# A graph layer on one Trainium2 core: a 16-bit table of places read in halves, and the residual input transferred behind the last super

## The chip, the cores and the metric

The kernel runs on one NeuronCore of a Trainium2 chip. The metric is device time in microseconds (us) of one execution; three executions of the kernel before gave 801.4, 800.42 and 801.16 us, median 801.16.

## The reference

There are 6250 nodes of 256 features (`x`) and 100,000 edges of 64 features. For every node the edges whose `src` it is are averaged; a two-layer MLP takes the node, this mean and a global vector; the result is added to `x` (the residual) and normalised.

```
sums   = segment_sum(edge_attr, src, 6250);  counts = segment_sum(1, src, 6250)
agg    = sums / max(counts, 1)
h      = relu(concat([x, agg, u[0]]) @ W1 + b1)          # hidden 512
out    = layernorm(x + h @ W2 + b2)                      # rows of 256
```

`dst` plays no part in the result.

## The kernel before, in words

All five engines have a program of their own, written out by hand, and meet at semaphores. The work has three stages.

**Sorting (to about 450 us).** Edges are taken in 44 chunks of 18 tiles of 128. TensorE sorts them with one-hot matmuls (L858) into groups of 4 edges of the same bucket (25 buckets of 250 nodes), ScalarE evacuates them, and GpSimd writes them with indirect DMAs (L600) to `sorted_rows` in HBM. Beside it TensorE makes the first layer's product of `x` (L785). VectorE works out a table `where` with two values per super (L1197 to L1220): its first half holds for each super the column in PSUM to which its sums go (the place, used by TensorE), its second half the row of `sorted_rows` at which each pair of supers begins (used by SyncE). SyncE writes it to HBM (L483) and reads it back as one row of one partition, `where_row` (L493), here with 32-bit elements.

**Supers (about 452 to 671 us).** A super is 128 rows of `sorted_rows`; there are 258, in 129 pairs. For each pair SyncE transfers 396 KB into one of 8 buffers `sup` (L511), as soon as TensorE is done with the pair that lay there (`s_added`, L510). VectorE compares node numbers for three or four of its four slots (L1236), ScalarE does the fourth slot of every second super (L713, L716): that gives `onehot`, of which there are 4 buffers. TensorE adds up each super with 24 matmuls of 64 or 65 columns, each with a weight load of its own (L936), into PSUM at a column that only the table knows. TensorE's program is a loop of 16 turns of 16 supers (`super_turn`, L926, called in the loop at L942 and once more at L944 for the last 2 supers). A turn starts with one `pe.load` of the 16 places into 16 registers (L927). In each super `pe.snap` makes an address of a register (L929), the sequencer waits for `s_hot_d` (L930) and in every second super for `s_hot_a` (L932), and the matmuls follow.

SyncE's program goes in turns of 8 pairs: `find_rows` loads 8 registers with the pairs' rows (L503), and 8 transfers follow. Turns 0 to 2 are written out, turns 3 to 14 are a loop (L524), turns 15 and 16 are written out again (turn 16 has one pair). The residual input `x` goes into `xs` in 12 pieces of 4 columns (two DMAs each, L527, behind the supers of turns 3 to 14) and a last one of 2 columns (L531, behind turn 15). `XPART` splits each piece into partitions 0 to 111 and 112 to 124.

**Output (about 671 us to the end).** 25 steps of two node columns: transposes of the means, the edges' part of layer one (L972, L974), relu on ScalarE, the second layer (L990), `y + xs` on VectorE (L1296), the moments, the normalisation on ScalarE (L748), and the store by SyncE (L538). Before `xs` is used, GpSimd adds `b2` to it (`add_b2`, L619); it does so for 3 steps ahead before the steps begin, and then for step g + 3 in step g. It waits once for all of `xs` (L614).

Of the kernel before, what the change touches and what calls it, by code (L numbers as in the profile page):

```python
# [9 lines left out]
I32 = mybir.dt.int32  # L10
U32 = mybir.dt.uint32
U16 = mybir.dt.uint16
# [5 lines left out]
P = 128  # L18
NODES, DIM = 6250, 256
# [5 lines left out]
NP = 125  # L25
COLS = NODES // NP
BUCKETS = COLS // 2
ROW = FEAT + 1
XPART = 112
# [35 lines left out]
SUPER_PAIRS = -(-SUPERS // 2)  # L65
ZERO_SUPER = 2 * SUPER_PAIRS
# [7 lines left out]
SUPER_COLS = -(-SUPERS // P)  # L74
# [19 lines left out]
PAIR_BUFS = 8  # L94
HOT_BUFS = 4
BODY = 2 * PAIR_BUFS
SUP_TURNS = SUPER_PAIRS // PAIR_BUFS
ACT_SLOT = SLOTS - 1
TURN = 3
TURNS = CHUNKS // TURN  # L100
# [5 lines left out]
LOOKS = -(-(BATCHES - SOON) // LOOK)  # L106
assert LOOKS + 3 <= CHUNKS

X_TURN = 3
X_COLS = 4  # L110
X_PIECES = COLS // X_COLS
X_PIECE = X_COLS * DIM
B2_AHEAD = 3
Z_BUFS = 3
assert X_TURN + X_PIECES + 1 == SUP_TURNS

STEPS = COLS // 2
PAIR = 10
# [4 lines left out]
def build(nc, x, src, attr, u, w1, b1, w2, b2, out):  # L123
# [1 line left out]
    first_d = nc.dram_tensor("first_d", [BATCHES, E1], U8, kind="Internal").ap()  # L125
    jump_d = nc.dram_tensor("jump_d", [BATCHES, E1], U16, kind="Internal").ap()
    clear_d = nc.dram_tensor("clear_d", [CLEARS * P], U32, kind="Internal").ap()
    where_d = nc.dram_tensor("where_d", [2, SUPER_COLS * P], I32, kind="Internal").ap()
    src_main = src[0:FULL * P].rearrange("(p t) -> p t", p=P)
    attr_main = attr[0:FULL * P, :].rearrange("(p t) f -> p (t f)", p=P)  # L130
    x_v = x.rearrange("(p c) d -> p (c d)", p=NP)
# [4 lines left out]
    with ctx:  # L136
        def sb(name, shape, dt=F32):
            return ctx.enter_context(nc.sbuf_tensor(name, shape, dt))

        def edge_sb(name, shape, dt=F32):  # L140
            return edge_ctx.enter_context(nc.sbuf_tensor(name, shape, dt))
# [4 lines left out]
        def sem(name):  # L146
            return ctx.enter_context(nc.semaphore(name))

        ident = sb("ident", [P, P])
        b2_all = sb("b2_all", [P, DIM])  # L150
        eps_col = sb("eps_col", [P, 1])
        where_row = sb("where_row", [1, 2 * SUPER_COLS * P], I32)
        node_of = sb("node_of", [P, 2 * P], I16)
        pre = sb("pre", [P, COLS * HID // P * NP])
        stats = sb("stats", [P, 2, 2, 6])
# [56 lines left out]
        bank_at = edge_sb("bank_at", [P, SUPER_COLS])  # L212
        column = edge_sb("column", [P, SUPER_COLS])
        beyond = edge_sb("beyond", [P, SUPER_COLS])
        where = edge_sb("where", [P, 2, SUPER_COLS], I32)
        chosen = edge_sb("chosen", [P, SOON * E1])
        edge_ctx.close()

# [56 lines left out]
        xs = sb("xs", [P, COLS * DIM])  # L275
# [88 lines left out]
        s_apart = sem("s_apart")  # L364
        s_added = sem("s_added")
        s_table = sem("s_table")
        s_xs = sem("s_xs")
        s_xb = sem("s_xb")
        s_own_act = sem("s_own_act")
        s_own_dve = sem("s_own_dve")  # L370
# [33 lines left out]
        def _(sp):  # L404
# [97 lines left out]
            def find_rows(m, count=PAIR_BUFS):  # L502
                sp.load(row_regs[0:count], where_row[0:1, bass.ds(m * PAIR_BUFS + SUPER_COLS * P, count)])  # L503

            def super_turn(m, count=PAIR_BUFS, found=False):
                if not found:
                    find_rows(m, count)
                for k in range(count):
                    at = sp.snap(row_regs[k], min_val=0, max_val=ZERO_SUPER * P)
                    sp.wait_ge(s_added, m * BODY + (2 * k + 2))  # L510
                    sp.dma_start(sup_pair[k][:, :, :, :].rearrange("p s r w -> p s (r w)"),  # L511
                                 sorted_rows[bass.ds(at, 2 * P), :].rearrange("(s p) w -> p s w", p=P)
                                 ).then_inc(s_sup[k], 16)
# [4 lines left out]
                sp.wait_ge(s_sent[s], 16 * CHUNKS)  # L518

            super_turn(0, found=True)  # L520
            for m in range(1, X_TURN):
                super_turn(m)
            sp.wait_ge(s_pre, COLS + 1)
            with sp.Fori(X_TURN, X_TURN + X_PIECES) as m:  # L524
                super_turn(m)
                for lo, hi in ((0, XPART), (XPART, NP)):
                    sp.dma_start(xs[lo:hi, bass.ds(m * X_PIECE - X_TURN * X_PIECE, X_PIECE)],  # L527
                                 x_v[lo:hi, bass.ds(m * X_PIECE - X_TURN * X_PIECE, X_PIECE)]).then_inc(s_xs, 16)
            super_turn(X_TURN + X_PIECES)
            for lo, hi in ((0, XPART), (XPART, NP)):  # L530
                sp.dma_start(xs[lo:hi, X_PIECES * X_PIECE:COLS * DIM], x_v[lo:hi, X_PIECES * X_PIECE:COLS * DIM]  # L531
                             ).then_inc(s_xs, 16)
            super_turn(SUP_TURNS, SUPER_PAIRS - SUP_TURNS * PAIR_BUFS)

            def store_step(g, b):
                sp.wait_ge(s_out, g * 2 + 2)
# [10 lines left out]
        def _(pool):  # L547
# [63 lines left out]
                pool.wait_ge(s_w_hi, 3)  # L611
                nc.gpsimd.tensor_tensor(low, whole, high.bitcast(F32), ALU.subtract).then_inc(s_w_lo, 1)
            pool.wait_ge(s_b2, 16)
            pool.wait_ge(s_xs, 2 * 16 * (X_PIECES + 1))  # L614

            def add_b2(g):
                for c in range(2 * g, 2 * g + 2):
                    column_x = xs[0:NP, c * DIM:(c + 1) * DIM]
                    nc.gpsimd.tensor_tensor(column_x, column_x, b2_all[0:NP, :], ALU.add).then_inc(s_xb, 1)  # L619

            for g in range(B2_AHEAD):
                add_b2(g)
# [9 lines left out]
            for g in range(STEPS):  # L632
                low_hidden(g, g % 2)
                if g + B2_AHEAD < STEPS:
                    add_b2(g + B2_AHEAD)

        @block.scalar
        def _(act):
# [70 lines left out]
            def super_turn(m, count=BODY):  # L709
                for k in range(0, count, 2):  # L710
                    act.wait_ge(s_sup[k // 2], m * 16 + 16)
                    act.wait_ge(s_added, m * BODY + (k + 1 + SUP_FREE - HOT_BUFS))
                    nc.scalar.activation(apart[k // 2 % 2][:, :], node_of[:, :], ACT.Abs, scale=-1.0,  # L713
                                         bias=place_in[k][:, ACT_SLOT, :]).then_inc(s_apart, 1)
                    act.wait_ge(s_apart, m * PAIR_BUFS + (k // 2 + 1))
                    nc.scalar.activation(onehot[k % HOT_BUFS][:, ACT_SLOT, :], apart[k // 2 % 2][:, :], ACT.Relu, scale=-1.0,  # L716
                                         bias=1.0).then_inc(s_hot_a, 1)

            with act.Fori(0, SUP_TURNS) as m:
                super_turn(m)  # L720
            super_turn(SUP_TURNS, 2 * SUPER_PAIRS - SUP_TURNS * BODY)

# [46 lines left out]
        def _(pe):  # L769
# [153 lines left out]

            table_regs = [pe.alloc_register(f"table_reg{k}") for k in range(BODY)]

            def super_turn(m, count=BODY):  # L926
                pe.load(table_regs[0:count], where_row[0:1, bass.ds(m * BODY, count)])  # L927
                for k in range(count):
                    at = pe.snap(table_regs[k], min_val=0, max_val=(PAIR_BANKS - 1) * 1024 + (BANK_COLS - 1) * ROW)  # L929
                    pe.wait_ge(s_hot_d, m * BODY + (k + 1))  # L930
                    if k % 2 == 0:
                        pe.wait_ge(s_hot_a, m * PAIR_BUFS + (k // 2 + 1))  # L932
                    for r in range(SLOTS):
                        for h in range(2):
                            for part, width in ((0, FEAT), (1, FEAT), (2, ROW)):
                                last = nc.tensor.matmul(ps[:, bass.ds(at + h * 512, width)],  # L936
                                                        onehot[k % HOT_BUFS][:, r, h * P:(h + 1) * P],
                                                        sup[k][:, r, part * PLANE:part * PLANE + width],
                                                        start=False, stop=False)
                    last.then_inc(s_added, 1)  # L940

            with pe.Fori(0, SUP_TURNS) as m:  # L942
                super_turn(m)
            super_turn(SUP_TURNS, 2 * SUPER_PAIRS - SUP_TURNS * BODY)  # L944
            for k in range(BANKS):
                last = nc.tensor.matmul(table_p[k], zeros[:, :], zeros[:, 0:1].to_broadcast([P, table_p[k].shape[1]]),
# [408 lines left out]
```

## Time and profile before

| | |
|---|---|
| runs | 801.4, 800.42, 801.16 us, median 801.16 |
| profiled execution's span, first to last instruction | 799.5 us |
| TensorE matmuls busy | 745.1 us, 93% of the span |
| VectorE busy | 716.8 us, 90% |
| ScalarE, GpSimd busy | 501.7 us, 63%; 417.1 us, 52% |
| HBM traffic | 195 GB/s over the span |
| stage of the supers | about 452 to 671 us |

The page does not say which of the three times belongs to the profiled execution; what lies around the span is 0.9 to 1.9 us. Busy shares are means over the three stages, and a matmul counts as busy from its start to its modelled end, so matmuls that are started 31 ns apart and are 193 ns long give a busy TensorE throughout. Times of single instructions on a sequencer (loads of registers, branches, waits) are not in the busy times; they have rows of their own, marked with a q (PEldq is TensorE's sequencer, SPq is SyncE's).

### The profile page before, as it was taken

What the parts mean: (1) busy time and instruction counts of PE and PEld (TensorE: products, weight loads), DVE (VectorE), ACT (ScalarE), POOL (GpSimd) and SP (SyncE); (2) the same over time, 40 slices, a digit from 0 to 9 for tenths busy, and PEclk for the clock granted to TensorE, in tenths of its full rate; (3) what the DMA queues carried; (4) which work ended last, traced back from release to release, by engine and by line L of the source; (5) the groups of instructions that cost most, each with busy time, mean ns of one, the idle gap of its engine ahead of it and who ended that gap; (6) DMA issues with size and microseconds to landing.
All of it is one profiled execution on the core that took longest, in us unless ns stands there. A gap on an engine that the chain in (4) does not pass through costs nothing.

```text
span 799.5 us, 31269 instructions
## 1 busy us (share of the span) xinstructions
PE 745.1 (93%) x11398; PEld 711.5 (89%) x11399; DVE 716.8 (90%) x2382; ACT 501.7 (63%) x998; POOL 417.1 (52%) x410
## 2 busy tenths in 40 slices
PE   8889999999999999999999888989898986899995
PEld 4689999999999999999999888989898986899995
DVE  8999999999999999999896388989898988799995
ACT  1366676666667767667667545555555552688886
POOL 3087777777677787877776400000000002788983
PEclk9999999999999999999999999999999999999999
DMA  6366556666665666656674678999999990012122
GB/s 215 131 210 204 201 202 211 213 215 219 202 219 195 212 220 211 225 205 214 203 210 167 239 227 260 281 282 282 285 283 285 281 277 10 27 52 64 53 66 64
DMA packets 75268, 156.38 MB, mean 196 GB/s; under 512 B 11084, under 2 KB 51277, under 8 KB 75097
## 3 DMA queue, kind: packets, MB, share of 16 engines
q1 hardware_dynamic: 58328, 102.33, 42.5%
q0 software_dynamic: 16896, 53.54, 17.9%
q8 instruction: 18, 0.29, 0.2%
q14 instruction: 26, 0.20, 0.1%
HBM read 95.47 MB, written 60.37 MB: 195 GB/s over the span
## 4 chain that ended last, share of the span: by engine, by line
PE 60%; DVE 30%; issue 5%; ACT 2%; POOL 1%; DMA 1%; DVEq 0%; ACTq 0%; SPq 0%; POOLq 0%
PE ps L858 33%; DVE onehot L1236 18%; PE ps L785 11%; PE ps L936 5%; PE ps L990 3%; DVE pre L1275 2%; DVE perm L1146 2%; DVE stats L1301 1%; DVE weights_z L1296 1%; PE ps L776 1%; PE ps L792 1%; POOL h_low L628 1%; PE ps L811 1%; PE ps L843 1%; PE ps L841 1%
## 5 line engine op out<-in xcount | busy, mean ns | idle before, releaser
L600 POOL DMA_INDIRECT sorted_rows<-payload,idx x264 | 304.8, 1155 | 131.8 <-issue 51.9
L858 PE MATMUL ps<-attr_buf,perm 128*128 128x198 bf16 x3168 | 302.6, 252 | 1.1 <-ACT attr_buf L642 0.8
L858 PEld LDWEIGHTS ps<-attr_buf,perm 128*128 128x128 bf16 x3168 | 288.6, 96 | 6.1 <-ACT attr_buf L642 1.2
L649 ACT CAST payload<-ps 128x792 bf16<-128x792 f32 x264 | 217.9, 825 | 76.7 <-PE ps L858 62.2
L1146 DVE TENSOR_SCALAR perm<-place_of,pos 128x512 bf16<-128x512 int16 x792 | 241.1, 362 | 3.4 <-PE ps L858 2.7
L1236 DVE TENSOR_SCALAR onehot<-node_of,sup 128x256 bf16<-128x256 int16 x903 | 192.4, 284 | 41.9 <-PE ps L936 22.3
L936 PE MATMUL ps<-sup,onehot 128*128 128x64 bf16 (+1 forms) x6192 | 196.1, 193 | 24.7 <-DVE onehot L1236 21.0
L936 PEld LDWEIGHTS ps<-sup,onehot 128*128 128x128 bf16 x6192 | 193.5, 98 | 27.3 <-issue 27.3
L619 POOL TENSOR_TENSOR xs<-xs,b_all 125x256 f32<-125x256 f32 x50 | 37.6, 775 | 209.4 <-DMA xs<-in_x 209.4
L713 ACT ACTIVATE apart<-node_of,sup 128x256 bf16<-128x256 int16 x129 | 65.6, 508 | 94.3 <-PE ps L936 90.2
L785 PE MATMUL ps<-xt,w1x 128*128 128x125 f32 x800 | 99.9, 278 | 5.9 <-DVE pos L1067 3.3
L785 PEld LDWEIGHTS ps<-xt,w1x 128*128 128x128 f32 x800 | 93.2, 192 | 10.8 <-issue 4.6
L660 ACT ACTIVATE pre<-ps,hid_bias 128x125 f32 (+1 forms) x200 | 56.7, 368 | 61.7 <-PE ps L785 61.7
L628 POOL TENSOR_TENSOR h_low<-pre,h_high 128x500 fp32r<-128x500 f32 x50 | 62.8, 1278 | 32.7 <-ACT pre L737 32.7
L1056 DVE TENSOR_TENSOR attr_buf<-attr_buf 128x576 f32<-128x576 f32 x88 | 65.8, 749 | 7.8 <-DMA attr_buf<-in_edge_attr 7.8
L1062 DVE TENSOR_TENSOR attr_buf<-attr_buf 128x576 f32<-128x576 f32 x88 | 65.4, 744 | 0.0
L716 ACT ACTIVATE onehot<-apart 128x256 bf16<-128x256 bf16 x129 | 53.8, 417 | 4.1
L990 PE MATMUL ps<-w_high,h_high 128*125 128x256 f32 x200 | 49.8, 282 | 1.0 <-issue 0.5
L990 PE MATMUL ps<-w_low,h_high 128*125 128x256 f32 x200 | 49.5, 280 | 0.0
L990 PE MATMUL ps<-w_high,h_low 128*125 128x256 f32 x200 | 34.1, 292 | 7.6 <-POOL h_low L628 7.6
L990 PEld LDWEIGHTS ps<-w_high,h_high 128*125 128x125 f32 x200 | 37.1, 185 | 1.3 <-issue 0.7
L990 PEld LDWEIGHTS ps<-w_low,h_high 128*125 128x125 f32 x200 | 37.2, 186 | 0.0
(150 smaller groups left out, 603.7 us busy)
## 6 DMA issues: line engine op xcount, KB each, us to landing
sup<-sorted_rows SPq DMA_DIRECT2D x129, 396.0 KB, 4.0
attr_buf<-in_edge_attr SPq DMA_DIRECT2D x43, 576.0 KB
out<-weights_z SPq DMA_DIRECT2D x25, 224.0 KB
xs<-in_x SPq DMA_DIRECT2D x12, 448.0 KB
x_stage<-in_x SPq DMA_DIRECT2D x47, 112.0 KB
sorted_rows<-payload,idx POOLq DMA_INDIRECT x264
pre<-jump_d SPq DMA_DIRECT2D x1, 1560.0 KB, 10.4
pre<-first_d SPq DMA_DIRECT2D x1, 780.0 KB, 7.2
```

The lines of the kernel that those rows point to most:

```text
L600: pool.indirect_dma_start(out=sorted_rows, out_offset=bass.IndirectOffsetOnAxis(ap=idx[:, n:n + 1], axis=0), in_=payload[s][:, :], in_offs ...
L628: nc.gpsimd.tensor_tensor(h_r[b][1][:, at:end], pre[:, g * KH * NW + at:g * KH * NW + end], h_r[b][0][:, at:end].bitcast(F32), ALU.subtrac ...
L649: nc.scalar.copy(payload[s][:, :].rearrange("p (r w) -> p r w", w=PART), slots_p[s % PSUM_BUFS]).then_inc(s_pay, 1)
L713: nc.scalar.activation(apart[k // 2 % 2][:, :], node_of[:, :], ACT.Abs, scale=-1.0, bias=place_in[k][:, ACT_SLOT, :]).then_inc(s_apart, 1)
L785: last = nc.tensor.matmul(pre_p[b][:, k * NP:(k + 1) * NP], w1x[:, c, k * P:(k + 1) * P], xt[b][:, c, :], start=(c == 0), stop=(c == KX - 1))
L858: last = nc.tensor.matmul(slot_p[s % PSUM_BUFS][r].rearrange("p (h f) -> p h f", f=PLANE), places, parts(a, t * CB + s), start=(t == 0 and ...
L936: last = nc.tensor.matmul(ps[:, bass.ds(at + h * 512, width)], onehot[k % HOT_BUFS][:, r, h * P:(h + 1) * P], sup[k][:, r, part * PLANE:pa ...
L990: last = nc.tensor.matmul(y_p[b][0:NP, c * DIM:(c + 1) * DIM], h_r[b][part][:, at:at + NP], w2r[w_part][:, k * DIM:(k + 1) * DIM], start=( ...
L1056: nc.vector.tensor_tensor(left, whole, high, ALU.subtract).then_inc(s_rest, 1)
L1062: nc.vector.tensor_tensor(low, left, middle, ALU.subtract).then_inc(s_low, 1)
L1146: last = nc.vector.tensor_scalar(perm[s][:, t, :], place_of[:, :], pos[:, bass.ds(c * CT + (t * CB + s), 1)], None, ALU.is_equal)
L1236: last = nc.vector.tensor_scalar(onehot[k % HOT_BUFS][:, r, :], node_of[:, :], place_in[k][:, r, :], None, ALU.is_equal)
```

## The change

The table `where`, its copy in HBM and `where_row` become 16-bit, and `where_row` is allocated first in SBUF. TensorE loads its places in halves of 8: the first half before the loop, then within each turn, ahead of super 4, the places of supers 8 to 15 of this turn, and ahead of super 12 the places of supers 0 to 7 of the next. A turn begins without a load, and the last 2 supers have none either. SyncE still loads 8 rows at the start of each turn, from the 16-bit table; its turns 1 to 15 are one loop, without DMAs of `xs` in it. Behind the last super SyncE issues `xs` in 5 pieces of 10 columns, two DMAs each, with a semaphore for each piece, and GpSimd waits for a piece when it comes to its first column.

```diff
+AHEAD = PAIR_BUFS // 2
...
-X_TURN = 3
-X_COLS = 4
+X_COLS = 10
...
-    where_d = nc.dram_tensor("where_d", [2, SUPER_COLS * P], I32, kind="Internal").ap()
+    where_d = nc.dram_tensor("where_d", [2, SUPER_COLS * P], U16, kind="Internal").ap()
...
+        where_row = sb("where_row", [1, 2 * SUPER_COLS * P], U16)
         ident = sb("ident", [P, P])
         b2_all = sb("b2_all", [P, DIM])
         eps_col = sb("eps_col", [P, 1])
-        where_row = sb("where_row", [1, 2 * SUPER_COLS * P], I32)
...
-        where = edge_sb("where", [P, 2, SUPER_COLS], I32)
+        where = edge_sb("where", [P, 2, SUPER_COLS], U16)
...
-        s_xs = sem("s_xs")
+        s_xs = [sem(f"s_xs{k}") for k in range(X_PIECES)]
...
             super_turn(0, found=True)
-            for m in range(1, X_TURN):
+            with sp.Fori(1, SUP_TURNS) as m:
                 super_turn(m)
+            super_turn(SUP_TURNS, SUPER_PAIRS - SUP_TURNS * PAIR_BUFS)
+
             sp.wait_ge(s_pre, COLS + 1)
-            with sp.Fori(X_TURN, X_TURN + X_PIECES) as m:
-                super_turn(m)
+            for k in range(X_PIECES):
                 for lo, hi in ((0, XPART), (XPART, NP)):
-                    sp.dma_start(xs[lo:hi, bass.ds(m * X_PIECE - X_TURN * X_PIECE, X_PIECE)],
-                                 x_v[lo:hi, bass.ds(m * X_PIECE - X_TURN * X_PIECE, X_PIECE)]).then_inc(s_xs, 16)
-            super_turn(X_TURN + X_PIECES)
-            for lo, hi in ((0, XPART), (XPART, NP)):
-                sp.dma_start(xs[lo:hi, X_PIECES * X_PIECE:COLS * DIM], x_v[lo:hi, X_PIECES * X_PIECE:COLS * DIM]
-                             ).then_inc(s_xs, 16)
-            super_turn(SUP_TURNS, SUPER_PAIRS - SUP_TURNS * PAIR_BUFS)
+                    sp.dma_start(xs[lo:hi, k * X_PIECE:(k + 1) * X_PIECE], x_v[lo:hi, k * X_PIECE:(k + 1) * X_PIECE]
+                                 ).then_inc(s_xs[k], 16)
...
-            pool.wait_ge(s_xs, 2 * 16 * (X_PIECES + 1))
...
             def add_b2(g):
+                if g % (X_COLS // 2) == 0:
+                    pool.wait_ge(s_xs[g // (X_COLS // 2)], 2 * 16)
                 for c in range(2 * g, 2 * g + 2):
...
+            def find_tables(half, at):
+                pe.load(table_regs[half * PAIR_BUFS:(half + 1) * PAIR_BUFS], where_row[0:1, bass.ds(at, PAIR_BUFS)])
+
             def super_turn(m, count=BODY):
-                pe.load(table_regs[0:count], where_row[0:1, bass.ds(m * BODY, count)])
                 for k in range(count):
+                    if k == PAIR_BUFS - AHEAD:
+                        find_tables(1, m * BODY + PAIR_BUFS)
+                    if k == BODY - AHEAD:
+                        find_tables(0, m * BODY + BODY)
                     at = pe.snap(table_regs[k], min_val=0, max_val=(PAIR_BANKS - 1) * 1024 + (BANK_COLS - 1) * ROW)
...
+            find_tables(0, 0)
             with pe.Fori(0, SUP_TURNS) as m:
                 super_turn(m)
```

## Rows read from the trace of the kernel before

**Rows 1.** The page: its first line and its busy times.
```profile
span 799.5 us, 31269 instructions
PE 745.1 (93%) x11398; PEld 711.5 (89%) x11399; DVE 716.8 (90%) x2382; ACT 501.7 (63%) x998; POOL 417.1 (52%) x410
```

**Rows 2.** Stretches without and with `xs`: engines' busy us, clock, DMA share, GB/s.
```profile
470.00:495.00 25.00, 23.73 (x767) 23.54 (x765) 22.59 (x108) 14.47 (x32) 0.00 (x0) 1.00 0.79 237
500.00:650.00 150.00, 136.01 (x4364) 134.70 (x4361) 133.69 (x637) 84.13 (x182) 0.00 (x0) 1.00 0.93 284
```

**Rows 3.** Timeline, TensorE's matmuls in the supers: start, us, idle before.
```profile
469.79 11.99 PE L936 MATMUL ps<-sup,onehot 128*128 128x64 bf16 x384 [1.29 <-DVE onehot L1236]
483.05 12.03 PE L936 MATMUL ps<-sup,onehot 128*128 128x64 bf16 x384 [1.27 <-DVE onehot L1236]
...
655.55 6.87 PE L936 MATMUL ps<-sup,onehot 128*128 128x64 bf16 x216 [1.29 <-DVE onehot L1236]
663.18 0.95 PE L936 MATMUL ps<-sup,onehot 128*128 128x64 bf16 x24 [0.76 <-DVE onehot L1236]
664.84 4.66 PE L936 MATMUL ps<-sup,onehot 128*128 128x64 bf16 x144 [0.70 <-DVE onehot L1236]
669.96 1.69 PE L936 MATMUL ps<-sup,onehot 128*128 128x64 bf16 x48 [0.47 <-DVE onehot L1236]
```

**Rows 4.** Timeline of one turn's boundary, 534.5 to 537.5 us, TensorE and VectorE.
```profile
534.23 1.56 DVE L1236 TENSOR_SCALAR onehot<-node_of,sup 128x256 bf16<-128x256 int16 x7
534.31 0.57 PE L936 MATMUL ps<-sup,onehot 128*128 128x65 bf16 x13
...
536.13 1.53 PE L936 MATMUL ps<-sup,onehot 128*128 128x64 bf16 x43 [1.25 <-DVE onehot L1236]
```

**Rows 5.** Same boundary, by source line: ns min/median/max, first and last start.
```profile
L942 PEldq COMPARE_BRANCH  x1: 208/208/208, 534.3 to 534.3; - x1
L942 PEldq FUSED_REGOPS  x1: 65/65/65, 534.5 to 534.5; - x1
...
L927 PEldq TENSOR_LOAD <-where_row x1: 1107/1107/1107, 534.7 to 534.7; - x1
...
L929 PEldq FUSED_REGOPS  x1: 41/41/41, 535.8 to 535.8; - x1
...
L929 PEldq FUSED_REGOPS  x1: 41/41/41, 536.4 to 536.4; - x1
...
L936 PE MATMUL ps<-sup,onehot x7: 191/193/194, 536.7 to 536.9; 128*128 128x64 bf16 x4, 128*128 128x65 bf16 x3
```

**Rows 6.** Register loads by source line, TensorE's L927 and SyncE's L503, by stretch.
```profile
L927 PEldq TENSOR_LOAD <-where_row x1: 1296/1296/1296, 450.8 to 450.8; - x1
...
L927 PEldq TENSOR_LOAD <-where_row x13: 1102/1106/1127, 481.6 to 640.7; - x13
...
L927 PEldq TENSOR_LOAD <-where_row x1: 556/556/556, 669.0 to 669.0; - x1
...
L503 SPq TENSOR_LOAD <-where_row x3: 533/537/538, 453.8 to 482.5; - x3
...
L503 SPq TENSOR_LOAD <-where_row x12: 691/696/706, 497.2 to 642.9; - x12
...
L503 SPq TENSOR_LOAD <-where_row x1: 507/507/507, 655.8 to 655.8; - x1
```

**Rows 7.** Timeline, VectorE over one turn of 16 supers.
```profile
510.55 11.93 DVE L1236 TENSOR_SCALAR onehot<-node_of,sup 128x256 bf16<-128x256 int16 x56 [1.33 <-PE ps L936]
```

**Rows 8.** Timelines of SyncE and GpSimd, 652 to 690 us; source line 1296; landing of L511.
```profile
657.41 0.41 SPq L511 DMA_DIRECT2D sup<-sorted_rows  x1
...
660.18 4.15 POOL L619 TENSOR_TENSOR xs<-xs,b_all 125x256 f32<-125x256 f32 x6 [209.40 <-DMA xs<-in_x]
...
L1296 DVE TENSOR_TENSOR weights_z<-ps,xs x50: 406/414/426, 686.6 to 793.4; 125x256 f32<-125x256 f32 x50
...
DMA to landing us min/median/max: 3.1/4.0/5.4
```

More of the change, by code:

```diff
@@ L97 @@
 SUP_TURNS = SUPER_PAIRS // PAIR_BUFS
+AHEAD = PAIR_BUFS // 2
+assert 2 * SUPER_PAIRS - SUP_TURNS * BODY <= PAIR_BUFS
+assert (ZERO_SUPER + 1) * P < 65536
 ACT_SLOT = SLOTS - 1
@@ L114 @@
 Z_BUFS = 3
-assert X_TURN + X_PIECES + 1 == SUP_TURNS
+assert X_PIECES * X_COLS == COLS and X_COLS % 2 == 0 and X_COLS // 2 >= B2_AHEAD
 STEPS = COLS // 2
```

## The prediction

> **What bounds the kernel now.** I read the page first. Its span is 799.5 us, 1.7 us under the median of the three runs, 801.16; the page does not say which of them it is, so differences are worked out in the span and put on the median. TensorE and VectorE are both busy for nine tenths of it [rows 1], so neither share says which of them sets the end. The change touches the stage of the supers only, from 452 to 671 us, and the hand-over of `xs` behind it; that stage is read by itself.
>
> The timeline of TensorE's matmuls shows there one block of 384 matmuls per turn, 12.0 us long, and then a hole of 1.25 to 1.3 us [rows 3]. The 384th ends 0.19 us after it starts, so starts are (11.99 − 0.19) / 383 = 30.8 ns apart, a super of 24 takes 0.74 us and a turn without holes 384 × 0.0308 = 11.83 us. Turns 1 and 15 start at 469.79 and 655.55 us: (655.55 − 469.79) / 14 = 13.27 us per turn. So each boundary costs 13.27 − 11.83 = 1.44 us, and there are 15 of them (into turns 1 to 15), 21.6 us. The last two supers start at 669.96 where 664.84 + 144 × 0.0308 = 669.28 was due, 0.7 us more [rows 3]. Together 22.3 us of the stage are holes at boundaries.
>
> The rows put the hole down to VectorE's `onehot`, and that is to be distrusted. VectorE's last instruction before the hole ends at 534.23 + 1.56 = 535.79 [rows 4]; it is then four one-hots ahead, and TensorE, which needs the first of them, starts only at 536.13. What TensorE's sequencer does in between has rows of its own [rows 5]: a branch at 534.3 (208 ns), an address step at 534.5 (65 ns), the load of 16 places at 534.7 (1107 ns), the first super's address at 535.8, the first matmul at 536.13. The load ends at 535.8 and nothing is issued before it does. The load is the hole.
>
> The engine doesn't feel all of the sequencer's time, since the sequencer runs ahead. The next super's address step is at 536.4, while the last matmul of the super before it starts at 536.9 [rows 5]: a lead of 0.50 us. It has the same size at each super of this turn, so 0.50 us is what any pause of the sequencer is forgiven.
>
> **Part 1: loads in halves.** Removed: 15 loads of 16 places and one of 2. Left at a boundary is the branch: it ends at 534.5, an address step follows 0.06 us later, and from there to the first matmul the rows have 536.13 − 535.83 = 0.30 us, so the matmul starts at 534.84 where 534.72 was due. That is 0.12 us for 15 boundaries, and about 0.1 us for the one into the last two supers: 1.9 us.
>
> Added: two loads of 8 places in each of 16 turns, 32 loads, and one before the loop. A load of T us in mid-turn adds its address step (0.12 us to the load's start), T and 0.06 us behind it; the step from address to matmul is 0.30 us, the lead gives back 0.50 and the due distance is 0.03: a hole of 0.12 + T + 0.06 + 0.30 − 0.50 − 0.03 = T − 0.05 us. "Half a turn ahead" takes away no more than this, because the sequencer stands still for the load wherever it is. Behind the load are queued the waits for `s_hot_d` and the matmuls; VectorE and SyncE wait for their `s_added`, and both only follow.
>
> The price T is what the trace doesn't show: 8 places of 16 bits, on TensorE. The nearest rows [rows 6]: TensorE takes 1106 ns for 16 and 556 ns for 2, both right behind a branch; on a straight line between them 8 cost 556 + 6 × 39 = 792 ns. SyncE takes 696 ns for 8 right behind a branch, 537 ns for 8 with no branch just before, and 507 ns for 1. The new loads have no branch before them, so the row of the same count and the same situation is 537; TensorE's load of 2 is 49 ns longer than SyncE's of 1, and I add most of that: **T = 0.58 us**. Ends: 0.507, and 0.792. Of 16 bits against 32 no row says anything; I give it nothing, and the lower end would go below 0.5 if the time goes by bytes.
>
> Holes after: 32 × (0.58 − 0.05) + 1.9 = 18.9 us. Gain 22.3 − 18.9 = 3.4 us. The break-even is at T = (22.3 − 1.9) / 32 + 0.05 = 0.69 us, inside the range of the rows: half the pieces, twice the number, and most of a load's time is not per place.
>
> [...]
>
> The first load, before the loop, takes 1296 ns for 16 [rows 6] and ends at 452.1. The matmuls start at 452.46 behind ScalarE's first one-hot too; I count at most 0.1 us, and nothing in the sum.
>
> **Part 2: what comes next if the holes shrink.** VectorE takes 11.93 us for a turn's 56 comparisons without a pause [rows 7]; the forecast period is 11.83 + 0.12 + 2 × 0.53 = 13.0 us, so VectorE has over 1 us of slack in a turn and doesn't show. The transfers of supers take 0.79 of the DMA engines without `xs` and land in 4.0 us (3.1 to 5.4) [rows 2, 8], with 8 buffers of 1.5 us each.
>
> **Part 3: `xs` out of the supers.** SyncE issues 24 fewer DMAs there. The turns without `xs` traffic run at 483.05 − 469.79 = 13.26 us, those with it at 13.27 on average [rows 3], though the DMA share goes from 0.79 to 0.93 [rows 2]. So taking it out gives nothing; the cover is the slack of the DMA engines, and it stays. SyncE's own loads and issues are shorter than a turn and follow `s_added`.
>
> Behind the supers: the last pair is issued at 657.41 [rows 8], since it waits for a buffer, and the ten DMAs follow from 657.9 on at some 0.5 us each. A piece is 125 × 10 KB = 1.28 MB, at 284 GB/s [rows 2] 4.5 us; behind 0.8 MB of the last pairs the first one lands near 665, the fifth near 683. VectorE reads `xs` first at 686.6 [rows 8] and the column of the fifth piece 20 steps of 4.4 us later. The stores come after. Nothing waits. GpSimd's six additions ahead ran from 660.18 for about 4.6 us and stretched VectorE's comparisons, with two holes of 0.7 to 0.76 us on TensorE [rows 3, 8]. Now they run near 665 to 669.5: still within the supers, so the same holes, some 1.8 us of starts, are paid again. Bounds: 1 us less if they fall behind VectorE's last comparison, 1 us more if they reach the chain of the means. I take 0.
>
> The 16-bit `where` costs VectorE two small writes as before, and its trip to HBM and back ends long before it is needed: nothing. **Sum:** 801.16 − 3.4 = 797.8 us.
>
> **Rivals.**
> A, the forecast: mid-turn loads cost 0.50 to 0.63 us, 5.9 to 1.8 us of gain, 795.3 to 799.4. Chance 0.45.
> B, loads as dear as SyncE's behind a branch: T = 0.70, holes 32 × 0.65 + 1.9 = 22.7, 801.6 us: the change only spreads the hole. For it: 12 of 16 of SyncE's loads take it. Against it: the 3 with no branch before. Chance 0.20 (T from 0.63 to 0.74).
> C, on the other side: the cost on TensorE goes by places, T = 0.79 at 8, holes 32 × 0.74 + 1.9 = 25.6 us, 804.5 us. It decides from T = 0.74 on. For it: TensorE's own two rows, and a read of 16 bits might be no cheaper than one of 32. Against it: SyncE's 1 and 8 lie 30 ns apart. Chance 0.27.
> D, loads all but hidden: if the sequencer could run 1.0 us ahead, a mid-turn load of 0.58 us would vanish, holes 2 us, 781 us. Against it: the lead of 0.50 us with nothing to wait for. The Trainium skill ("TensorE: Matmul & The Clock Gate", section on the array's architecture, engine queue depths) gives TensorE's queue 64 entries, which would be 32 matmuls with their weight loads, 0.99 us of lead as an estimate; the trace has half of it. Chance 0.03.
> E, T under 0.5 because 16 bits halve the time per place: 32 × 0.40 + 1.9 = 14.7, 793.6 us. Chance 0.05.
>
> **The numbers.** The likeliest is A, 797.8 us. A measurement of this kernel can tell about 0.2%, 1.6 us, from no change: T below 0.63 is faster, above 0.74 slower. Faster: A, D, E, 0.52 with the little that the adds may take. Same 0.20, slower 0.28. The range reaches from T = 0.507 with 0.5 us off at the adds (794.8) to C (804.6).
>
> **What would show it.** In the profile after: 33 loads on TensorE, their median is T; two holes per turn in its timeline, ahead of supers 4 and 12, of T − 0.2 us by the profile's way of counting from a matmul's end, and none at the boundary; a period near 13.0 us; the block of VectorE unbroken at 11.9 us. `xs` landing behind 660 with GpSimd's additions before 670, VectorE's first read of `xs` shifted by no more than the gain. It is wrong if the median is over 0.69, if holes of another cause take their place (VectorE's comparisons, `sup` landing late), or if step 0 of the output waits for GpSimd.

## The result, and the profile after

The changed kernel takes 841.62 us (median of 4 runs, 840.65 to 841.85) against 800.79 us for the kernel before measured beside it (800.39 to 801.4, 4 runs): ratio 1.0501, 95% interval 1.0485 to 1.0518. It is 41 us slower, where 3.4 us faster was forecast, and far outside the range. The profiled execution of the changed kernel took 840.65 us.

The page of the kernel after, its first line and busy times (compare [rows 1]):

```profile
span 838.6 us, 31246 instructions
PE 752.1 (90%) x11398; PEld 714.1 (85%) x11399; DVE 721.4 (86%) x2382; ACT 501.1 (60%) x998; POOL 412.2 (49%) x410
```

The span grew by 39.1 us. TensorE's and VectorE's busy times grew by 7 and 5 us only, so most of the growth is waiting. The next view is the timeline of TensorE's matmuls in the supers (compare [rows 3]); the number in brackets is the idle time before the block, the hole:

```profile
454.38 4.63 PE L941 MATMUL ps<-sup,onehot 128*128 128x64 bf16 x96 [2.27 <-DVE onehot L1242]
...
476.23 6.08 PE L941 MATMUL ps<-sup,onehot 128*128 128x64 bf16 x192 [1.69 <-DVE onehot L1242]
484.01 6.31 PE L941 MATMUL ps<-sup,onehot 128*128 128x64 bf16 x192 [1.71 <-DVE onehot L1242]
...
697.42 6.13 PE L941 MATMUL ps<-sup,onehot 128*128 128x64 bf16 x192 [1.76 <-DVE onehot L1242]
705.24 3.96 PE L941 MATMUL ps<-sup,onehot 128*128 128x64 bf16 x120 [1.69 <-DVE onehot L1242]
709.89 0.94 PE L941 MATMUL ps<-sup,onehot 128*128 128x64 bf16 x24 [0.69 <-DVE onehot L1242]
```

The blocks are of 192 matmuls, 8 supers, where they were of 384, with a hole of 1.7 us ahead of each. They begin at supers 4 and 12, where the new loads are. A turn takes (697.42 − 476.23) / 14 = 15.80 us instead of 13.27. The boundary itself is no hole any more, only 0.23 us by which the block with the branch in it is longer (6.31 against 6.08).

The loads of registers from `where_row`, TensorE's L926 and SyncE's L505 (compare [rows 6]):

```profile
L926 PEldq TENSOR_LOAD <-where_row x33: 1917/1924/2112, 451.8 to 703.0; - x33
L505 SPq TENSOR_LOAD <-where_row x17: 266/1661/2214, 435.7 to 693.3; - x17
```

A load of 8 places from the 16-bit table takes 1924 ns on TensorE and 1661 ns on SyncE; a load of 16 places from the 32-bit one took 1106 ns on TensorE. SyncE's fastest, 266 ns, is the one of a single row.

VectorE shows the same holes and is not their cause; its blocks of 28 comparisons wait for TensorE each time (its timeline):

```profile
508.79 6.01 DVE L1242 TENSOR_SCALAR onehot<-node_of,sup 128x256 bf16<-128x256 int16 x28 [1.81 <-PE ps L941]
```

The stretch from 500 to 650 us, with the DMA engines at 0.70 instead of 0.93 (compare [rows 2]):

```profile
500.00:650.00 150.00, 117.56 (x3649) 114.25 (x3646) 113.79 (x532) 70.30 (x152) 0.00 (x0) 1.00 0.70 204
```

The hand-over of `xs`, timelines of SyncE and GpSimd (compare [rows 8]):

```profile
694.79 5.51 SPq L530 DMA_DIRECT2D xs<-in_x  x10
...
705.13 4.15 POOL L618 TENSOR_TENSOR xs<-xs,b_all 125x256 f32<-125x256 f32 x6 [253.13 <-DMA xs<-in_x]
```

VectorE's use of `xs`, by source line:

```profile
L1302 DVE TENSOR_TENSOR weights_z<-ps,xs x50: 406/415/427, 726.2 to 832.4; 125x256 f32<-125x256 f32 x50
```

GpSimd starts 10.3 us behind the first issue and is done with its six additions, at 709.3 us, long before VectorE first reads `xs` at 726.2.

**The sum.** From the first super matmul to the end of the last the stage takes 710.83 − 454.38 = 256.5 us, before 671.65 − 452.46 = 219.2: 37.3 us more. It starts 1.9 us later. That is 39.2 of the span's 39.1 us; the output behind the stage is as long as before.

### The profile page after: what moved, and what is told of

Its sections match the earlier page's. It is cut to its first block, busy times and chain, and to the rows that moved or that the text cites. A ratio compares the mean times of both kernels' runs of the same rounds, so it can differ in the third digit from the quotient of the medians.

```text
span 838.6 us, 31246 instructions
## 1 busy us (share of the span) xinstructions
PE 752.1 (90%) x11398; PEld 714.1 (85%) x11399; DVE 721.4 (86%) x2382; ACT 501.1 (60%) x998; POOL 412.2 (49%) x410
## 4 chain that ended last, share of the span: by engine, by line
PE 61%; DVE 25%; issue 7%; ACT 2%; DMA 2%; POOL 1%; DVEq 0%; ACTq 0%; SPq 0%; POOLq 0%
PE ps L857 29%; DVE onehot L1242 13%; PE ps L941 13%; PE ps L784 9%; PE ps L996 4%; DVE perm L1152 3%; DVE pre L1281 2%; DMA sorted_rows<-payload,idx 2%; POOL h_low L627 1%; DVE stats L1307 1%; DVE weights_z L1302 1%; PE ps L791 1%; DVE attr_buf L1068 1%; PE ps L810 1%; ACT h_high L731 1%
## 5 line engine op out<-in xcount | busy, mean ns | idle before, releaser
L598 POOL DMA_INDIRECT sorted_rows<-payload,idx x264 | 299.8, 1136 | 138.0 <-ACT payload L648 54.4
L1242 DVE TENSOR_SCALAR onehot<-node_of,sup 128x256 bf16<-128x256 int16 x903 | 194.9, 284 | 78.4 <-PE ps L941 57.6
L941 PE MATMUL ps<-sup,onehot 128*128 128x64 bf16 (+1 forms) x6192 | 201.6, 194 | 57.1 <-DVE onehot L1242 57.0
L941 PEld LDWEIGHTS ps<-sup,onehot 128*128 128x128 bf16 x6192 | 195.9, 98 | 62.9 <-issue 61.2
L659 ACT ACTIVATE pre<-ps,hid_bias 128x125 f32 (+1 forms) x200 | 56.5, 367 | 61.7 <-PE ps L784 61.6
```

Source lines behind the costliest of these rows:

```text
L598: pool.indirect_dma_start(out=sorted_rows, out_offset=bass.IndirectOffsetOnAxis(ap=idx[:, n:n + 1], axis=0), in_=payload[s][:, :], in_offs ...
L1242: last = nc.vector.tensor_scalar(onehot[k % HOT_BUFS][:, r, :], node_of[:, :], place_in[k][:, r, :], None, ALU.is_equal)
```

## The experiments

They ran on other chips, where the kernel before took 844 to 849 us. What is longer there is the sorting (the first super starts at 493 to 505 us instead of 452), by amounts that differ from run to run; a turn of the stage of supers is the same to 0.01 us where the loads are those of before (e3, e5). So beside each ratio to the kernel before on the same chip I give the stage, first super matmul to end of the last, from one profile each (219.2 us before). The stage has the first turn in it, and that one differs by a few us from run to run: in e7 and e8 the first unbroken block of 384 matmuls took 13.4 us (in e7 the granted clock from 520 to 530 us is 0.83), where e8's later ones took 12.1 at 1.00. The period, the time from one turn to the next, is free of this.

| run | table, loads per turn | TensorE's load, ns | period, us | stage, us | ratio (95%) |
|---|---|---|---|---|---|
| before | 32 bits, 1 of 16 | 1106 | 13.27 | 219.2 | 1 |
| after | 16 bits, 2 of 8 | 1924 | 15.80 | 256.5 | 1.0501 (1.0485 to 1.0518) |
| e1_i32_halves | 32 bits, 2 of 8 | 590 | 13.13 | 215.0 | 0.9903 (0.9866 to 0.994) |
| e2_u16_only | 16 bits, 1 of 16 | 3790 | 17.24 | 277.4 | 1.0704 (1.0662 to 1.0747) |
| e3_xs_only | 32 bits, 1 of 16 | 1106 | 13.27 | 216.7 | 0.9935 (0.9901 to 0.9969) |
| e4_u16_quarters | 16 bits, 4 of 4 | 987 | 15.87 | 259.2 | 891 us against 849, one run |
| e5_row_first | 32 bits, 1 of 16 | 1107 | 13.27 | 218.7 | 0.9996 (0.9959 to 1.0034) |
| e6_mid_super | 32 bits, 2 of 8 | 590 | 12.66 | 206.2 | 0.9832 (0.9765 to 0.9899) |
| e8_one_load | 32 bits, 1 of 16 | 1110 | 12.85 | 212.7 | 0.9905 (0.9871 to 0.994) |
| e7_packed | 8 words of 32 bits | 592 | 12.71 | 209.7 | 0.9901 (0.986 to 0.9941) |
| e9_packed_ahead | 8 words of 32 bits | 592 | 12.42 | 204.2 | 0.9888 (0.985 to 0.9926) |
| e10_mid_super | as e6_mid_super | 590 | 12.67 | 207.1 | 0.99 (0.9864 to 0.9936) |

All but e2 and e5 have `xs` behind the supers. The theory to be tested, W: the price is the 16-bit element of the load. The rival, P: it is where the load stands or where the row lies.

### e1_i32_halves: the width taken back

```diff
-        where_row = sb("where_row", [1, 2 * SUPER_COLS * P], U16)
+        where_row = sb("where_row", [1, 2 * SUPER_COLS * P], I32)
```

(`where_d` and `where` likewise; all else as after.)

> The changed kernel with the table of places in 32 bits again; halves, first allocation in SBUF and xs behind the supers stay. Theory W (the element's width is the price of a load): TensorE's loads of 8 fall from 1.92 us to 0.54 to 0.79 us, the holes from 32 x 1.87 + 1.9 = 61.8 us to 17.6 to 25.6 us, the time to 796 to 805 us. Rival P (a load in mid-turn, beside running matmuls, or from the first bytes of a partition, is dear): the loads stay near 1.9 us, the time near 841 us.

The loads, by tile:

```profile
L926 PEldq TENSOR_LOAD <-where_row x33: 587/590/775, 498.2 to 709.3; - x33
L505 SPq TENSOR_LOAD <-where_row x17: 282/523/1097, 478.9 to 701.0; - x17
```

TensorE's timeline from super 4 of turn 1 and of turn 15:

```profile
519.85 6.18 PE L941 MATMUL ps<-sup,onehot 128*128 128x64 bf16 x192 [0.35 <-ACT onehot L715]
...
703.73 6.13 PE L941 MATMUL ps<-sup,onehot 128*128 128x64 bf16 x192 [0.35 <-ACT onehot L715]
```

Same places, same positions, same first bytes of the partition: the load of 8 falls from 1924 to 590 ns, the hole from 1.7 to 0.35 us. P is out and W stands. 0.59 us is also what the prediction took for T (0.58). The stage is 4.2 us shorter than before, near the forecast gain of 3.4, but not by the forecast's terms alone: the period fell by 0.13 us, not by 0.27, which is 2.1 us in 16 turns, and most of the rest is the move of `xs`, which the prediction put at nothing (e3 below).

### e2_u16_only: the width alone

The kernel before with `where_d`, `where` and `where_row` in U16, one load of 16 at the head of a turn.

> The kernel before with the table in 16 bits and nothing else: one load of 16 places at the head of a turn, where_row at its old place in SBUF, xs among the supers. Theory W: a load of 16 places costs about twice the 1.92 us of 8, 3.7 to 3.9 us instead of 1.11, so 15 boundaries cost 2.7 us more each, about 41 us, time about 842 us; SyncE's loads of 8 near 1.66 us as in the changed kernel. Rival P: loads 1.1 us, time as before, 801 us.

The loads, by tile:

```profile
L503 SPq TENSOR_LOAD <-where_row x17: 473/1824/2257, 479.8 to 763.3; - x17
L927 PEldq TENSOR_LOAD <-where_row x17: 526/3790/4007, 500.8 to 780.0; - x17
```

A stretch of the stage (busy times, granted clock, DMA share, GB/s):

```profile
560.00:700.00 140.00, 108.34 (x3120) 107.39 (x3117) 95.35 (x451) 60.27 (x130) 0.00 (x0) 0.89 0.73 217
```

Two single microseconds of the block that begins at 663.24 us:

```profile
664.00:665.00 1.00, 1.00 (x23) 1.00 (x21) 0.25 (x2) 0.25 (x1) 0.00 (x0) 0.50 0.24 74
666.00:667.00 1.00, 1.00 (x38) 1.00 (x36) 0.95 (x5) 0.19 (x1) 0.00 (x0) 1.00 0.00 0
```

The width alone makes loads of 16 cost 3790 ns instead of 1106, and is enough to make the kernel 7% slower. The time rose by more than expected, 58 us in the stage, not 41: 2.68 us × 15 = 40 are the loads, and the granted clock in the stretch from 560 to 700 us (the column behind the busy times) is 0.89 where it was 1.00 [rows 2]. The 0.89 is a mean of two levels: at the head of a block the clock is 0.50 (1.2 GHz, 23 matmuls started in a microsecond), then 1.00 (2.4 GHz). Blocks of 384 matmuls took 13.1 to 14.7 us instead of 12.0. TensorE had stood idle for 3.9 to 4.0 us before each; with holes of 1.7 us (after) the clock stayed at 1.00. The period shows the same split: 17.24 − 13.27 = 3.97 us, of which 2.68 are the load and 1.29 the slower matmuls. That such idle time can cost clock besides is a second price of a long load. SyncE's loads took 1824 ns and not the 1660 expected: here the `xs` DMAs stand before them again (see "A wrong reading without effect on the outcome").

### e4_u16_quarters: price by place or by load

```diff
+            QUART = PAIR_BUFS // 2
...
-                    if k == PAIR_BUFS - AHEAD:
-                        find_tables(1, m * BODY + PAIR_BUFS)
-                    if k == BODY - AHEAD:
-                        find_tables(0, m * BODY + BODY)
+                    if k % QUART == QUART - 2:
+                        q = k // QUART + 1
+                        find_tables(q % 4, m * BODY + q * QUART)
```

> The changed kernel with four loads of 4 places per turn instead of two of 8 (16 bits, 64 loads in the loop). Theory W with a price by place: SyncE's 1 place took 0.27 us and 8 took 1.66 us, so about 0.2 us a place; TensorE's 8 took 1.92 us, so 4 cost about 1.0 us, holes 64 x 0.95 + 1.9 = 63 us, time 840 to 845 us. Rival, a price by load: each stays near 1.9 us, holes 64 x 1.87, time near 900 us.

The loads, by tile:

```profile
L928 PEldq TENSOR_LOAD <-where_row x65: 982/987/1176, 501.6 to 758.0; - x65
L505 SPq TENSOR_LOAD <-where_row x17: 266/1661/1922, 479.8 to 745.8; - x17
```

4 places take 987 ns, 8 take 1924 and 16 take 3790, on TensorE: 234 ns for each place between 4 and 8, 233 between 8 and 16, and only some 50 ns beside them; e2's load of 2 places, 526 ns, fits this too. SyncE pays (1661 − 266) / 7 = 199 ns. In 32 bits 8 places cost 34 ns more than 2 (590 against 556 [rows 6]). In 16 bits the price is by place; in 32 bits, up to 8 places, TensorE's is nearly all by load. The stage comes out at 259.2 us, about as long as with halves, as a price by place wants it. The total, 891 us, is higher than I had written since the chip's sorting was longer, which the expectation had not reckoned with.

The Trainium skill ("Runtime: NRT & Kernel Launch", section on instruction fetch mechanics) puts a load of registers at about 200 ns for each register, even in bulk; it speaks there of loads that the runtime adds. In this kernel's loads from SBUF the rows on SyncE and TensorE agree with it for 16-bit elements (199 and 233 ns) and not for 32-bit ones.

### e3_xs_only: the transfers alone

The kernel before (32 bits, load of 16 at the head) with the change's edits to SyncE's program and GpSimd's waits.

> The kernel before with only xs moved behind the last super in five pieces. My theory: nothing, within 1 us of the kernel before; the period of a turn stays 13.27 us, the two holes from GpSimd's additions stay. Rival: among the supers xs cost something (SyncE's issues, a busier DMA system, slower register loads on SyncE): the period falls below 13.2 us, or behind them it costs something: the first steps of the output wait for GpSimd and the time rises by over 1.6 us.

Timelines of TensorE (first and last whole turn, then the end), VectorE and GpSimd:

```profile
516.42 11.99 PE L932 MATMUL ps<-sup,onehot 128*128 128x64 bf16 x384 [1.29 <-DVE onehot L1232]
...
702.16 12.06 PE L932 MATMUL ps<-sup,onehot 128*128 128x64 bf16 x384 [1.31 <-DVE onehot L1232]
714.66 1.70 PE L932 MATMUL ps<-sup,onehot 128*128 128x64 bf16 x48 [0.44 <-issue]
...
703.15 10.50 DVE L1232 TENSOR_SCALAR onehot<-node_of,sup 128x256 bf16<-128x256 int16 x49 [1.38 <-PE ps L932]
...
714.00 4.14 POOL L615 TENSOR_TENSOR xs<-xs,b_all 125x256 f32<-125x256 f32 x6 [215.27 <-DMA xs<-in_x]
```

The period is 13.27 us, as before: within the turns `xs` cost nothing, in spite of the busier DMA engines. Half of the expectation fails at the end: the last turn is one block of 384, without the two holes of 0.7 us that GpSimd's additions tore into it [rows 3]. VectorE's last comparison ends at 703.15 + 10.50 = 713.65 and the additions start at 714.00; they come too late to slow it. Nor do they delay what follows: from the last super matmul to the first read of `xs` it is 731.70 − 716.36 = 15.34 us, and in e5, with `xs` among the supers as before, 726.92 − 711.57 = 15.35 (15.0 in the profile of before). The stage is 2.5 us shorter. From the start of turn 15 to the start of the last two supers it is 714.66 − 702.16 = 12.50 us instead of 669.96 − 655.55 = 14.41: 1.9 us are the holes. The rest lies in the first turn, which takes 16.80 us here, 16.87 in e5 and 17.33 before, so it is none of the transfers'. So the transfers' move gains about 1.9 us. The ratio, 0.9935, leans the same way; its interval is too wide to give the size.

### e5_row_first: where the row begins

```diff
+        where_row = sb("where_row", [1, 2 * SUPER_COLS * P], I32)
         ident = sb("ident", [P, P])
...
-        where_row = sb("where_row", [1, 2 * SUPER_COLS * P], I32)
```

> The kernel before, 32 bits, one load of 16 places at the head of a turn; only the allocation of where_row is moved to the first bytes of its partition. Theory A (the step from 0.59 us for 8 places to 1.11 us for 16 comes from where the row begins): the load falls to about 0.62 us, a boundary costs 0.94 instead of 1.42 us, the period falls from 13.26 to about 12.8 us, 7 us in all. Rival N (it comes from the number, 8 being a limit): 1.11 us, period 13.26 us, no difference.

TensorE's loads, by tile:

```profile
L927 PEldq TENSOR_LOAD <-where_row x17: 548/1107/1297, 491.3 to 708.9; - x17
```

Nothing moved, ratio 0.9996. The step from 590 ns for 8 places to 1107 for 16 has to do with their number (or their 64 bytes), not with where the row begins. The two holes at the end are there again (at 703.1 and 704.75 us), `xs` being back among the supers.

### e6_mid_super and e10_mid_super: a load in the middle of a super

This is e1 (halves in 32 bits) with both loads taken from the head of their super and put behind its 12th matmul:

```diff
...
                     for r in range(SLOTS):
+                        if r == SLOTS // 2 and k == PAIR_BUFS - AHEAD:
+                            find_tables(1, m * BODY + PAIR_BUFS)
+                        if r == SLOTS // 2 and k == BODY - AHEAD:
+                            find_tables(0, m * BODY + BODY)
                         for h in range(2):
```

> The 32-bit kernel with halves (e1_i32_halves), each load issued behind the 12th matmul of its super instead of ahead of its first. My theory of the lead: ahead of a super the load adds to the 0.3 us of address step and waits, in the middle it meets a sequencer that is about 0.45 us ahead and has 12 matmuls to get ahead again, so a hole of T - 0.27 = 0.32 us in place of 0.52, period 12.7 us in place of 13.12, 6 us less than e1_i32_halves. Rival: the place within a turn makes no difference, period 13.1 us.

TensorE's loads, by tile:

```profile
L926 PEldq TENSOR_LOAD <-where_row x33: 587/590/777, 499.3 to 701.7; - x33
```

TensorE's timeline from the middle of super 4 of turn 1 and of turn 15:

```profile
518.95 6.04 PE L941 MATMUL ps<-sup,onehot 128*128 128x64 bf16 x192 [0.22 <-issue]
...
696.14 6.08 PE L941 MATMUL ps<-sup,onehot 128*128 128x64 bf16 x192 [0.16 <-issue]
```

The load is as long as in e1, 590 ns, but its hole falls from 0.35 to 0.16 us as the timeline counts it (add 0.16 for the time from a matmul's last start), and the period from 13.13 to 12.66 us. The expectation says why: the lead is used twice, once at the load, and once more, when 12 matmuls have given part of it back, at the next super's address and waits. This is the account of the prediction (a pause of the sequencer minus its lead), carried one step further. The hole comes out at 0.16 + 0.16 = 0.32 us, as expected, and the period at 12.66 us, where 12.7 was expected; how the lead builds up again behind the load was not read from the trace.

> e6_mid_super once more, with more rounds, on the same chip as e9_packed_ahead: period 12.65 us, stage of the supers 206 us, some 4 us more than e9_packed_ahead if one load of 8 words in place of two of 8 places is worth its hole of 0.33 us, 16 times; and 13 us less than the kernel before.

It gave 0.99 (0.9864 to 0.9936) and a stage of 207.1 us; e6's 0.9832, with an interval up to 0.9899, was on the lucky side. The turns agree to 0.01 us.

### e8_one_load, e7_packed and e9_packed_ahead: fewer loads

e8 takes the places of supers 14 and 15 first and loads all 16 of the next turn in the middle of super 14, still in 32 bits.

> As e6_mid_super, with one load of 16 places per turn, behind the 12th matmul of super 14, once the places of supers 14 and 15 are taken. Theory N, 1.11 us for 16: hole 0.84, boundary 0.14, period 12.9 us. Theory A, 0.62 us: hole 0.35, period 12.4 us. A rival for both: a hole there meets the boundary's and the sequencer has not caught up, period 0.2 us longer than these.

TensorE's loads, by tile:

```profile
L926 PEldq TENSOR_LOAD <-where_row x17: 1103/1110/1284, 497.7 to 708.2; - x17
```

Its timeline from the middle of super 14 of turns 1 and 15:

```profile
529.43 12.17 PE L944 MATMUL ps<-sup,onehot 128*128 128x64 bf16 x384 [0.71 <-issue]
...
709.35 2.79 PE L944 MATMUL ps<-sup,onehot 128*128 128x64 bf16 x84 [0.69 <-issue]
```

One load of 1110 ns with a hole of 0.70 us is worse than two of 590 with 0.16: period 12.85 against 12.66 us.

e7 keeps the table in 16 bits and loads it as 32-bit words.

```diff
+            where_words = where_row[:, :].bitcast(I32)
...
+                pe.load(table_regs, where_words[0:1, bass.ds(at, BODY // 2)])
...
+                if k % 2:
+                    pe.reg_alu(place_reg[1], table_regs[k // 2], 16, ALU.logical_shift_right)
+                else:
+                    pe.reg_alu(place_reg[0], table_regs[k // 2], 65535, ALU.bitwise_and)
```

> As e8_one_load, but the table lies in memory in 16 bits and is loaded as 32-bit words, 8 words for 16 places, each taken apart by one register operation of the sequencer; SyncE loads 4 words for 8 rows. Theory W says that the element of the load is the price, not what lies in memory: the load takes 0.59 us, hole 0.32, period 12.4 us, about 14 us less than the kernel before on the same chip. Rivals: the loads are dear again since the row is 16-bit (1.9 us); or the register operations use up the sequencer's lead and each super runs longer than 0.74 us.

The loads, by tile:

```profile
L509 SPq TENSOR_LOAD <-where_row x17: 286/299/573, 483.0 to 701.0; - x17
L938 PEldq TENSOR_LOAD <-where_row x17: 588/592/779, 503.2 to 711.1; - x17
```

TensorE's timeline at the end of turn 1 and the start of turn 2:

```profile
533.87 1.27 PE L960 MATMUL ps<-sup,onehot 128*128 128x64 bf16 x36 [0.37 <-issue]
535.35 10.89 PE L960 MATMUL ps<-sup,onehot 128*128 128x64 bf16 x348 [0.21 <-DVE onehot L1261]
```

This settles W: the memory holds 16-bit places, and 16 of them are loaded in 592 ns, because the load's element is a word. The time did not follow the expectation: the period is 12.71 us, not 12.4. The hole at the load was 0.34 to 0.40 us instead of the 0.16 of e6, and a second one of up to 0.2 us opened at the boundary. The operations that take a word apart stand there in the sequencer's program, where the lead is needed; that they are the cause is what e9 tries. So e9 takes each place from its word two supers ahead, behind the 12th matmul.

> As e7_packed, with each place taken from its word two supers ahead, in the middle of a super, so that the load of 8 words in super 14 finds the sequencer's full lead. If e7_packed lost 0.2 us at the load and 0.2 us at the boundary to its register operations crowding there: hole 0.33, boundary 0.16, period 12.35 us, stage of the supers near 202 us, 17 us less than the kernel before. Rival: the extra operation in every super costs more lead than a super's 24 matmuls give back; then supers run longer than 0.74 us, or VectorE, which needs 11.93 us a turn, sets the period.

TensorE's timeline from the middle of super 14 of turns 1 and 15:

```profile
524.41 12.15 PE L959 MATMUL ps<-sup,onehot 128*128 128x64 bf16 x384 [0.27 <-issue]
...
698.26 2.83 PE L959 MATMUL ps<-sup,onehot 128*128 128x64 bf16 x84 [0.25 <-issue]
```

One hole of 0.25 us per turn, period (698.26 − 524.41) / 14 = 12.42 us, stage 204.2 us, 15 us less than before; 0.9888 (0.985 to 0.9926). The hole at the boundary is gone, and that at the load is smaller than in e7 but larger than expected (0.25 + 0.16 = 0.41 us, expected 0.33), which no run explains. By its ratio this kernel is ahead of both, with 832.34 us against 843.51 for the one before on that chip. Against e10 on the same chip (833.44 us) it is ahead in the stage, by 2.9 us, but not by the times, whose spread is larger.

## Why the prediction was wrong

**The reading of the stage held.** The hole at the boundary was the load, not VectorE: with the load gone from it, the hole is gone too. TensorE's sequencer stood still for a load in mid-turn as well, and about 0.50 us of each pause was forgiven. A mid-turn load of T was to cost T − 0.05 us: after, a hole of 1.70 + 0.19 − 0.03 = 1.86 for T = 1.92, and in e1 0.51 for 0.59, so T − 0.06 to T − 0.08. The boundary left 0.23 us by the blocks' lengths, not 0.12. Had T been known, the prediction's own formula gives 32 × (1.92 − 0.05) + 1.9 = 61.7 us of holes, 39.4 us more than before, 840.6 us; measured 841.62. That it comes so near is in part luck, since errors cancel:

- In the 14 turns from turn 1 to turn 15 the formula gives 33.9 us and the timeline 14 × 2.53 = 35.4, since the boundary costs more than was taken.
- In the rest of the stage the formula gives 5.5 us and the timeline shows 1.8. The kernel before had two holes of 1.0 and 1.1 us in its first turn (lines below) that the changed one does not show, for a reason that was not looked for, and one of the two holes from the additions is gone.
- The stage starts 1.9 us later, which the sum does not have.

```profile
461.51 3.86 PE L936 MATMUL ps<-sup,onehot 128*128 128x64 bf16 x119 [1.01 <-issue]
466.47 2.03 PE L936 MATMUL ps<-sup,onehot 128*128 128x64 bf16 x57 [1.10 <-issue]
```

**The step that failed** is the price of the load: "Of 16 bits against 32 no row says anything; I give it nothing". T was put at 0.58 us with ends at 0.507 and 0.792; it is 1.92, also far above the 0.69 us that the prediction had named as its sign of being wrong. With 32-bit elements it would have been right, 0.59. The ends were taken from rows of loads of another element, and the range was built on them, though no row bounded the new one from above. The only direction in which I let the width work was a cheaper load (rival E, "16 bits halve the time per place"); C mentioned that a 16-bit read "might be no cheaper". The opposite case, each place paid for by itself, had no rival, and a plain one was at hand: 8 places at the price of 8 separate loads. Why 16-bit elements are paid for one by one no run shows; the runs show that they are. SyncE's single 32-bit load of 507 ns could have served as its price, with up to 8 × 0.5 = 4 us at the far end.

**A wrong reading without effect on the outcome.** I took SyncE's 696 against 537 ns for the effect of a branch in front. In e1 and e3 its loads of 8 follow the loop's branch as well and take 523 and 525 ns at the median. What the dear ones had in common was the `xs` DMAs issued right before them. The load of a single row shows it too: the 507 ns of [rows 6] stand behind the last `xs` DMAs with no branch between, and without these DMAs it takes 282 ns in e1 and 286 in e3. So rival B stood on the wrong cause, and so did two readings that used 507 as if nothing stood before it: the lower end of T, and "SyncE's 1 and 8 lie 30 ns apart". Without the DMAs they lie 282 and 523 ns high, 240 apart.

**Terms set too small.** The first load was to gain at most 0.1 us and was put at nothing. It took 2112 ns instead of 1296 and ended at 453.9 instead of 452.1. Of the 1.9 us by which the first super is late, 0.8 are this load; the rest was there before it, since TensorE's last matmul ahead of it stands at 451.82 instead of 450.60. The boundary was put at 0.12 us and costs 0.23, also in e1 (6.36 against 6.13).

**`xs`.** "So taking it out gives nothing" is right within the turns to 0.01 us. The additions were expected to collide as before, 7 us behind the first issue. They started 10.3 us behind it, and 9.5 us in e3, where they fell behind VectorE's last comparison. That is the case which the prediction's bounds gave as "1 us less", found to be about 1.9 us. In the changed kernel the stage ends later, the additions still fall into it, and one hole of 0.69 us is left of the two. The move of `xs` is thus a gain of 1 to 2 us hidden under a loss of 41.

## What to carry to other kernels

When an edit changes the element of an operation, the rows of the old element bound nothing: say so, and put the far end where each element pays for itself. A load into registers held TensorE's whole program here. The best of the tried forms issues it as 32-bit words, unpacks them with register operations, and puts it in the middle of a long run of matmuls, with no other sequencer work next to it. The hole that it leaves is its length plus what surrounds it, less the sequencer's lead. Worked out from the rows this held to a tenth of a microsecond wherever nothing else stood next to the load; in e7, where the unpacking did, it was 0.2 us off. And rows are comparable only if what stands before them is: two DMAs ahead of a load made it 160 to 230 ns longer.

## What the runs showed of the hardware

- A load of registers from SBUF in 16-bit elements costs 233 ns a place on TensorE and 199 ns on SyncE. In 32-bit elements SyncE took 282 ns for 1, 299 for 4 and 523 for 8; TensorE 556 for 2, 590 for 8 and 1107 for 16. The price does not rise evenly. Where the row begins has no part in it (e5); what it follows was not found.
- SyncE's loads of 8 took 696 ns right behind two DMAs of `xs` and 523 without them, in 16 bits 1824 and 1661; the load of a single place took 507 and 282, in 16 bits 473 and 266. Why was not tried.
- TensorE's granted clock stayed at 1.00 with holes of 1.7 us every 7.9 us, and was 0.89 with holes of 3.9 us every 17 us, a mean of 1.2 GHz at the head of a block and 2.4 GHz behind it.
- GpSimd's six additions of 125 × 256 cost TensorE 1.9 us when they ran beside VectorE's comparisons (up to 769 ns for one of these, 278 at the median), and nothing that the profiles show when they ran just behind them.
